# Three rotating PSUM banks for the attention scores, with the bank of the K and V projections given up, in an attention and feed-forward layer on eight cores

## The chip, the cores and the metric

The kernel runs on the 8 cores of one Trainium2 chip. Each core computes two of the sixteen sequences with the same program, and no core talks to another. The metric is the device time of the slowest core in microseconds (us).

## The reference

```python
# x: (16, 2048, 1024); 16 query heads, 2 key/value heads of 64
q = (x @ Wq + bq).reshape(b, s, 16, 64).transpose(0, 2, 1, 3)
k = (x @ Wk + bk).reshape(b, s, 2, 64).transpose(0, 2, 1, 3)
v = (x @ Wv + bv).reshape(b, s, 2, 64).transpose(0, 2, 1, 3)
kp, vp = pad(k, 128 zeros on both sides), pad(v, likewise)
# position i sees the 256 padded positions i .. i+255
scores = einsum('bgrsd,bgswd->bgrsw', qg, k_win)
probs  = softmax(scores, axis=-1)
out    = einsum('bgrsw,bgswd->bgrsd', probs, v_win) @ Wo + bo
x = layernorm(x + out)
# complex linear layer, W_real and W_imag (512 x 512) unfolded from small factors
out_real = x_real @ W_real.T - x_imag @ W_imag.T + bias_real
out_imag = x_real @ W_imag.T + x_imag @ W_real.T + bias_imag
x = layernorm(x + concatenate([out_real, out_imag], axis=-1))
```

## The kernel before

**Order of the work.** One Python function, `schedule`, is run once for each engine and emits that engine's instructions in the order in which the units are called. Every engine therefore executes the same list of units in order, each taking from it only its own part. Synchronisation is by counting semaphores: a unit waits for the count that an earlier unit left under a name in `E.res(...)` or `E.ev[...]`. An instruction that waits holds up everything behind it on its engine.

**Stages.** For each of the two sequences (b = 0, 1) of 2048 rows:

- `emit_qkv(b, q)` handles 512 rows. It loads x in four blocks of 128 rows, converts them on ACT (L371), transposes them on PE (L381), copies the result with DVE (L391), and makes the queries in eight groups of eight matmuls (L411) into two PSUM banks pW0 and pW1 in turn, each evicted by ACT (L420). Then come the keys (L434, evicted at L440) and the values (L447, evicted at L454), both in the single bank pB, and four small transposes of the values (L464, L470). It is called for q = 0 and 1 ahead of the loop, for q = 2 at the end of iteration 5 and for q = 3 at the end of iteration 9: 8 calls in all.
- The main loop runs over k = 0 to 17, one block of 128 rows per iteration, as a software pipeline of three blocks: scores and exponentials of block S = k, attention output and its projection of block P = k - 1, feed-forward layer of block k - 2.

**One iteration on PE**: scores (0,0); values quad 0; scores (0,1); values quad 1; transposes of x1 (L735); feed-forward half 0 (L764); scores (1,0); values quad 2; feed-forward half 1; scores (1,1); values quad 3; transposes of the attention output (L612); scores (2,0); projection half 0 (L637); scores (2,1); projection half 1. The pair in brackets is (c, pair): c is one of three blocks of keys, pair one of two groups of heads.

**The score units.** `sc_unit` (L505) is two matmuls of 64 rows by 512 columns, one for each key/value head, in rows 0 to 63 and 64 to 127 of the array, into the banks pS0 and pS1. Each of the two waits for the exponential that last read its bank, the one of the unit just before. The unit signals once, at its second matmul. `exp_unit` (L523) is two ACT activations of 128x512, the first on pS0, the second on pS1; the first of them waits for the unit's signal. `av_unit` (L562) uses pS2 and pS3, which DVE empties (`recip_unit` L580, `normts_unit` L590).

**What stands on ACT between iterations.** `rstd1_unit` (L697, L702) computes the reciprocal deviation of the first layer norm of block P at the end of the iteration, from statistics that DVE makes (L680, L650 to L660) out of both projection halves. On ACT it stands ahead of the exponentials (0,0) of the next iteration. `x1norm_unit` (L715, DVE) follows it, and the transposes L735 of the next iteration wait for that.

**PSUM.** All 8 banks are in use: pS0 to pS3, pW0 and pW1, pB, pT.

Of the kernel before, what the change touches and what calls it, by code (L numbers as in the profile page):

```python
# [7 lines left out]
F32 = mybir.dt.float32  # L8
BF16 = mybir.dt.bfloat16
AF = mybir.ActivationFunctionType  # L10
# [4 lines left out]
TQ = 512  # L15
# [3 lines left out]
def build_nc(debug=False):  # L19
    nc = bass.Bass("TRN2", target_bir_lowering=False)  # L20
# [41 lines left out]
    KT = sb("KT", [128, 2304], BF16)  # L62
    VB = sb("VB", [128, 18 * 130], BF16)
    EX = sb("EX", [128, 24 * 512], BF16)
    vstage = sb("vstage", [128, 512], BF16)
# [14 lines left out]
    wk_sb = sb("wk_sb", [128, 1024], BF16)  # L80
    wv_sb = sb("wv_sb", [128, 1024], BF16)
# [7 lines left out]
    bk_sb = sb("bk_sb", [128, 1], F32)  # L89
    bv_sb = sb("bv_sb", [128, 1], F32)  # L90
# [4 lines left out]
    expbias = sb("expbias", [128, 1], F32)  # L95
# [16 lines left out]
    f2s = sb("f2s", [128, 512], BF16)  # L112
    wstage = [sb("wstage0", [128, D], F32)]

    pS = [nc.alloc_psum_tensor(f"pS{i}", [128, 512], F32).ap() for i in range(4)]
    pW = [nc.alloc_psum_tensor(f"pW{i}", [128, 512], F32).ap() for i in range(2)]
    pB = nc.alloc_psum_tensor("pB", [128, 512], F32).ap()
    pT = nc.alloc_psum_tensor("pT", [128, 1024], BF16).ap()

    SEMS = ["t", "s", "v", "g", "dc", "db", "dw0", "dw1", "dx0", "dx1", "do0", "do1"]  # L120
# [34 lines left out]
    def ap3(base_ap, offset, dims):  # L155
        return AP(base_ap.tensor, offset, dims)

    def schedule(E):
# [195 lines left out]
        def emit_qkv(b, q):  # L354
# [43 lines left out]
            def rhsXT(c):  # L398
                return ap3(XT, c * 128, [[4096, 128], [1024, 4], [1, 128]])

            ev_xt_ready = E.res("XT")["r"]
            for t in range(8):
# [22 lines left out]
                if t == 7:  # L425
                    rqt["r"] = ev_ev
                    rqt["f"] = None
            rb = E.res("pB")
            if cur == "t":
                E.wait(rb["f"])  # L430
                if b == 0 and q == 0:
                    E.wait(wconv_ev["wv"])
            for c in range(8):
                i = ten.matmul(pB[:, :], wk_sb[:, c * 128:(c + 1) * 128], rhsXT(c),  # L434
                               start=(c == 0), stop=(c == 7)) if cur == "t" else None
            ev_mm = E.inc("t", i if cur == "t" else None)
            if cur == "s":
                E.wait(ev_mm)
                E.wait(E.res("KTfree")["f"])
                i = sca.add(KT[:, 128 + q * TQ: 128 + (q + 1) * TQ], pB[:, :], bk_sb[:])  # L440
            ev_kev = E.inc("s", i if cur == "s" else None)
            rb["f"] = ev_kev
            E.res(f"KT{q}")["r"] = ev_kev
            if cur == "t":
                E.wait(rb["f"])
            for c in range(8):
                i = ten.matmul(pB[:, :], wv_sb[:, c * 128:(c + 1) * 128], rhsXT(c),  # L447
                               start=(c == 0), stop=(c == 7)) if cur == "t" else None
            ev_vmm = E.inc("t", i if cur == "t" else None)
            E.res("XTfree")["f"] = ev_vmm  # L450
            if cur == "s":
                E.wait(ev_vmm)
                E.wait(E.res("vstage")["f"])
                i = sca.add(vstage[:], pB[:, :], bv_sb[:])  # L454
            ev_vev = E.inc("s", i if cur == "s" else None)
            rb["f"] = ev_vev
            rpt = E.res("pT")
            ev_vbev = None
            for T in range(4):
# [17 lines left out]
            E.res(f"VB{q}")["r"] = ev_vbev  # L477

        quadcol = {0: 0, 1: 512, 2: 256, 3: 768}

        def sc_unit(b, S, c, pair):
            parity = (S // 4) % 2
            kb = S - 1 + c
            qready = E.res(f"QT{parity}")["r"]
            kready = E.res(f"KT{S // 4}")["r"]
            knext = E.res(f"KT{min(S // 4 + 1, 3)}")["r"]
            i = None
            for gq in range(2):
                quad = pair * 2 + gq
                rowbase = 64 * gq  # L490
                tilegrp = pair * 2048
                if cur == "t":
                    if gq == 0:
                        if b == 0 and S == 0 and c == 0:
                            E.wait(ev_init_v)
                        if debug and b == 0 and S in (1, 2) and c == 0 and pair == 0:
                            E.wait(E.ev.get("dbg0"))
                        E.wait(qready)
                        E.wait(kready)
                        E.wait(knext)  # L500
                    E.wait(E.res(f"scb{quad % 2}")["f"])
                rhs = ap3(QT, rowbase * 8192 + parity * 4096 + tilegrp
                          + (S % 4) * 128, [[8192, 64], [512, 4], [1, 128]])
                lhsT = KT[rowbase:rowbase + 64, (kb + 1) * 128:(kb + 2) * 128]
                i = ten.matmul(pS[quad % 2][:, :], lhsT, rhs, start=True, stop=True,  # L505
                               tile_position=(rowbase, 0)) if cur == "t" else None
            ev_sc = E.inc("t", i if cur == "t" else None)
            E.ev[f"sc_{S % 2}_{c}_{pair}"] = ev_sc
            if S % 4 == 3 and c == 2 and pair == 1:
                E.res(f"QT{parity}")["f"] = ev_sc  # L510

        def exp_unit(b, S, c, pair):
            ev_sc = E.ev[f"sc_{S % 2}_{c}_{pair}"]
            for gq in range(2):
                quad = pair * 2 + gq
                exi = (S % 2) * 12 + c * 4 + quad
                rex = E.res(f"exfree{exi}")
                if cur == "s":
                    if b == 0 and S == 0 and c == 0 and pair == 0 and gq == 0:
                        sca.wait_ge(SEMH["v"], ev_init_v[1])  # L520
                    E.wait(ev_sc)
                    E.wait(rex["f"])
                    i = sca.activation(EX[:, exi * 512:(exi + 1) * 512],  # L523
                                       pS[quad % 2][:, :], AF.Exp, bias=expbias[:])
                ev_e = E.inc("s", i if cur == "s" else None)
                E.ev[f"exp_{S % 2}_{c}_{quad}"] = ev_e
                if gq == 1:
                    E.res(f"scb0")["f"] = E.ev[f"exp_{S % 2}_{c}_{pair * 2}"]
                    E.res(f"scb1")["f"] = ev_e

        def mask_unit(b, S, c, pair):
            m = maskl if c == 0 else maskr
# [10 lines left out]

        def av_unit(b, S, quad):
            g = quad % 2
            bank = 2 + quad % 2
            vready = E.res(f"VB{S // 4}")["r"]
            vnext = E.res(f"VB{min(S // 4 + 1, 3)}")["r"]
            if cur == "t":
                E.wait(E.res(f"avb{quad % 2}")["f"])  # L550
                E.wait(vready)
                E.wait(vnext)
                for c in range(3):
                    key = ("msk" if c != 1 else "exp") + f"_{S % 2}_{c}_{quad}"
                    E.wait(E.ev[key])
            first = True
            i = None
            for c in range(3):
                kb = S - 1 + c
                exi = (S % 2) * 12 + c * 4 + quad  # L560
                for hh in range(4):
                    i = ten.matmul(  # L562
                        pS[bank][:, hh * 65:(hh + 1) * 65],
                        EX[:, exi * 512 + hh * 128: exi * 512 + (hh + 1) * 128],
                        VB[:, (kb + 1) * 130 + g * 65: (kb + 1) * 130 + (g + 1) * 65],
                        start=first, stop=(c == 2 and hh == 3)) if cur == "t" else None
                    first = False
            ev = E.inc("t", i if cur == "t" else None)
            E.ev[f"av_{S % 2}_{quad}"] = ev
            for c in range(3):  # L570
                E.res(f"exfree{(S % 2) * 12 + c * 4 + quad}")["f"] = ev

        def recip_unit(b, S, quad):
            ring = S % 2
            i = None
            if cur == "v":
                E.wait(E.ev[f"av_{S % 2}_{quad}"])
                if quad == 0:
                    E.wait(E.res(f"attn{ring}")["f"])
                i = vec.reciprocal(Rrec[:, ring * 16 + quad * 4: ring * 16 + (quad + 1) * 4],  # L580
                                   ap3(pS[2 + quad % 2], 64, [[512, 128], [65, 4]]))
            E.inc("v", i)

        def normts_unit(b, S, quad):
            ring = S % 2
            bank = 2 + quad % 2
            E.bar("v")
            i = None
            for hh in range(4):
                i = vec.tensor_scalar(  # L590
                    attn[:, ring * 1024 + quadcol[quad] + hh * 64:
                         ring * 1024 + quadcol[quad] + (hh + 1) * 64],
                    ap3(pS[bank], hh * 65, [[512, 128], [1, 64]]),
                    Rrec[:, ring * 16 + quad * 4 + hh: ring * 16 + quad * 4 + hh + 1],
                    None, ALU.mult) if cur == "v" else None
            ev_nq = E.inc("v", i)
            E.res(f"avb{quad % 2}")["f"] = ev_nq
            if quad == 3:
                E.res(f"attn{ring}")["r"] = ev_nq
                E.ev[f"nq_{ring}"] = ev_nq  # L600
# [403 lines left out]
```

How the kernel before makes its waits and increments, by code:

```python
        def bar(self, name):  # L139
            if self.cur == name:
                self.h.wait_ge(SEMH[name], self.c[name])
# [1 line left out]
        def wait(self, ev):  # L143
            if ev is None:
                return
            if isinstance(ev, list):
                for e in ev:
                    self.wait(e)
                return
            self.h.wait_ge(SEMH[ev[0]], ev[1])
# [7 lines left out]
    def schedule(E):  # L158
# [3 lines left out]
        vec = E.h if cur == "v" else None  # L162
        gps = E.h if cur == "g" else None
        syn = E.h if cur == "sync" else None
        if cur == "v":
            vec.memset(expbias[:], -32.0)
            vec.memset(neghalf[:], -0.5)
            vec.memset(ones_row[:], 1.0)
            i = vec.memset(VB[:], 0.0)
            i.then_inc(SEMH["v"], 1)
            vec.wait_ge(SEMH["v"], E.c["v"] + 1)
            vec.memset(ap3(VB, 64, [[2340, 128], [130, 18]]), 1.0)
            vec.memset(ap3(VB, 129, [[2340, 128], [130, 18]]), 1.0)
            vec.memset(KT[:, 0:128], 0.0)
# [22 lines left out]
        E.inc("db", i, 16)  # L198
        i = syn.dma_start(brow_st[0:1, :], bo_d.rearrange("(o f) -> o f", o=1)) \
            if cur == "sync" else None
        ev_bo = E.inc("db", i, 16)
        if cur == "s":
            sca.wait_ge(SEMH["db"], ev_bo[1])
            i = sca.copy(bo_row[:], brow_st[:])
        ev_borow = E.inc("s", i if cur == "s" else None)
        if cur == "sync":
            syn.wait_ge(SEMH["s"], ev_borow[1])
        i = syn.dma_start(brow_st[0:1, 0:512], br_d.rearrange("(o f) -> o f", o=1)) \
```

## Time and profile before

| | |
|---|---|
| runs of the kernel before | 1432.85 and 1475.86 us, median 1454.35 |
| profiled execution, its own time | 1431.67 us |
| its span, slowest core (core 3) | 1430.1 us |
| spans of the eight cores | 1425.3 to 1430.1 us |
| mean granted TensorE clock | 0.737 to 0.739 of full speed on all cores |
| PE busy / DVE / ACT / POOL | 60% / 37% / 28% / 25% of the span |

The span runs from the first to the last instruction of the slowest core. The engines are PE (TensorE matmul), PEld (its weight loads), DVE (VectorE), ACT (ScalarE), POOL (GpSimd) and SP. In a row of the timeline the first number is the start and the second the duration, both in us, "x2" is a count of merged instructions, and the bracket gives the idle time of the engine just before and the instruction that ended it.

### The profile page before, as it was taken

How to read it: one execution, taken by the hardware profiler on the slowest of the kernel's cores; microseconds unless marked ns; L12 is line 12 of the kernel's file. 1: busy time of each engine (PE TensorE's matmuls, PEld its weight loads, DVE VectorE, ACT ScalarE, POOL GpSimd, SP SyncE). 2: the span in 40 equal slices, each digit the busy share in tenths (PEclk: the TensorE clock that was granted, in tenths of full speed). 3: DMA queues.
4: the chain of work that ended last, by engine and by line, in shares of the span. 5: the costliest groups of instructions: out<-in, count | busy, mean ns of one | idle time of the engine just before them, and what ended most of it. 6: DMA issues, size and time to landing. Idle time of an engine off the chain costs nothing.

```text
span 1430.1 us, 17008 instructions; the slowest of 8 cores (1425.3 to 1430.1 us)
## 1 busy us (share of the span) xinstructions
PE 863.3 (60%) x4568; PEld 354.3 (25%) x4568; DVE 532.2 (37%) x1539; ACT 397.0 (28%) x673; POOL 357.8 (25%) x324
## 2 busy tenths in 40 slices
PE   0077334675586666676756576667577658666664
PEld 0033001222232223222222232222232223222221
DVE  0010444355414551444554111454425441455443
ACT  2332113223223223323220234322232322322210
POOL 0000004243213340333430104343214321333410
PEclk9997555677677677777676686767787767767676
DMA  4510000000200011000000300000200020000000
GB/s 128 177 66 24 0 1 0 1 27 18 74 1 16 16 34 55 16 16 15 15 31 15 104 30 1 15 16 16 74 1 30 15 74 1 15 16 30 15 16 30
DMA packets 15869, 44.51 MB, mean 31 GB/s; under 512 B 3091, under 2 KB 5539, under 8 KB 15782
## 3 DMA queue, kind: packets, MB, share of 16 engines
q0 software_dynamic: 9216, 33.56, 6.4%
q1 hardware_dynamic: 6566, 9.87, 2.4%
q8 instruction: 45, 0.74, 0.2%
q14 instruction: 42, 0.34, 0.1%
HBM read 26.65 MB, written 16.78 MB: 30 GB/s over the span
## 4 chain that ended last, share of the span: by engine, by line
PE 54%; DVE 19%; issue 11%; DMA 7%; ACT 6%; POOL 2%; DVEq 1%; SPq 0%; ACTq 0%; POOLq 0%
PE pW L764 12%; PE pW L637 11%; PE pW L411 9%; PE pS L505 5%; PE pS L562 4%; DVE scr L650 4%; DVE attn L590 4%; DMA xs<-x 4%; PE pT L735 2%; ACT EX L523 2%; PE pW L641 2%; PE pW L768 2%; DVE pre L783 2%; PE pT L612 2%; DVE pre L680 1%
## 5 line engine op out<-in xcount | busy, mean ns | idle before, releaser
L523 ACT ACTIVATE EX<-pS,expbias 128x512 bf16<-128x512 f32 x384 | 243.0, 684 | 395.5 <-PE pS L505 395.2
L539 POOL TENSOR_TENSOR EX<-EX,maskr_s 128x512 bf16<-128x512 bf16 x128 | 172.2, 1368 | 358.8 <-ACT EX L523 358.2
L539 POOL TENSOR_TENSOR EX<-EX,maskl_s 128x512 bf16<-128x512 bf16 x128 | 149.5, 1196 | 383.4 <-ACT EX L523 383.3
L637 PE MATMUL pW<-wo_sb,attnT 128*128 128x512 bf16 x512 | 180.3, 516 | 37.1 <-DVE pre L783 35.9
L505 PE MATMUL pS<-QT,KT 64*128 64x512 bf16 x384 | 120.4, 490 | 122.1 <-ACT EX L523 120.3
L411 PE MATMUL pW<-XT,wq_sb 128*128 128x512 bf16 x512 | 129.5, 420 | 8.9 <-DVE XT L391 8.9
L381 PE MATMUL pT<-identb,x_tm 128*128 128x128 bf16 x256 | 31.6, 301 | 150.5 <-ACT x_tm L371 134.3
L590 DVE TENSOR_SCALAR attn<-pS,Rrec 128x64 bf16<-128x64 f32 x512 | 110.2, 278 | 14.3 <-DVE attn L590 0.5
L764 PE MATMUL pW<-wrt,x1T 128*128 128x512 bf16 x256 | 92.5, 500 | 36.8 <-DVE Rrec L580 34.6
L650 DVE SCALAR_TENSOR_TENSOR scr<-pre 128x1024 bf16<-128x1024 f32 x64 | 102.3, 1598 | 6.7
L580 DVE RECIPROCAL Rrec<-pS 128x4 f32<-128x4 f32 x128 | 19.6, 172 | 205.8 <-PE pS L562 205.8
L637 PEld LDWEIGHTS pW<-wo_sb,attnT 128*128 128x128 bf16 x512 | 57.3, 122 | 142.3 <-issue 123.6
L562 PE MATMUL pS<-VB,EX 128*128 128x65 bf16 x1536 | 82.5, 213 | 5.5 <-POOL EX L539 2.2
L470 DVE COPY VB<-pT 128x128 bf16<-128x128 bf16 x32 | 7.3, 228 | 191.9 <-PE pT L464 191.9
L562 PEld LDWEIGHTS pS<-VB,EX 128*128 128x128 bf16 x1536 | 66.5, 109 | 46.6 <-issue 46.6
L420 ACT ACTIVATE QT<-pW,bq_sb 128x512 bf16<-128x512 f32 x64 | 44.1, 688 | 113.9 <-PE pW L411 113.9
L411 PEld LDWEIGHTS pW<-XT,wq_sb 128*128 128x128 bf16 x512 | 53.6, 106 | 83.0 <-issue 34.5
L612 PE MATMUL pT<-identb,attn 128*128 128x128 bf16 x256 | 23.6, 246 | 79.9 <-DVE attn L590 79.9
L391 DVE COPY XT<-pT 128x1024 bf16<-128x1024 bf16 x32 | 22.1, 691 | 133.0 <-PE pT L381 133.0
L505 PEld LDWEIGHTS pS<-QT,KT 64*128 64x128 bf16 x384 | 24.3, 97 | 189.6 <-issue 187.2
L680 DVE SCALAR_TENSOR_TENSOR pre<-pW,x_tm 128x512 f32<-128x512 f32 x64 | 44.0, 687 | 52.8 <-PE pW L641 52.8
L381 PEld LDWEIGHTS pT<-identb,x_tm 128*128 128x128 bf16 x256 | 24.1, 135 | 157.6 <-issue 157.6
(81 smaller groups left out, 787.6 us busy)
## 6 DMA issues: line engine op xcount, KB each, us to landing
xs<-x POOLq DMA_DIRECT2D x32, 512.0 KB, 4.4
y<-outst POOLq DMA_DIRECT2D x32, 512.0 KB, 3.0
wstage<-wq SPq DMA_DIRECT2D x4, 512.0 KB, 4.2
xs<-wq SPq DMA_DIRECT2D x4, 512.0 KB, 4.8
wstage<-wo SPq DMA_DIRECT2D x4, 512.0 KB, 4.1
xs<-wo SPq DMA_DIRECT2D x4, 512.0 KB, 4.1
wstage<-wk SPq DMA_DIRECT2D x1, 512.0 KB, 5.3
xs<-wv SPq DMA_DIRECT2D x1, 512.0 KB, 4.9
```

What stands on the lines that cost most here:

```text
L381: i = ten.transpose(pT[:, c * 128:(c + 1) * 128], x_tm[:, slot * D + c * 128: slot * D + (c + 1) * 128], identb[:]) if cur == "t" else None
L411: i = ten.matmul(pW[bank][:, :], wq_sb[:, c * 1024 + t * 128: c * 1024 + (t + 1) * 128], rhsXT(c), start=(c == 0), stop=(c == 7)) \
L505: i = ten.matmul(pS[quad % 2][:, :], lhsT, rhs, start=True, stop=True, tile_position=(rowbase, 0)) if cur == "t" else None
L523: i = sca.activation(EX[:, exi * 512:(exi + 1) * 512], pS[quad % 2][:, :], AF.Exp, bias=expbias[:])
L539: i = gps.tensor_mul(EX[:, exi * 512:(exi + 1) * 512], EX[:, exi * 512:(exi + 1) * 512], m[:]) \
L562: i = ten.matmul(pS[bank][:, hh * 65:(hh + 1) * 65], EX[:, exi * 512 + hh * 128: exi * 512 + (hh + 1) * 128], VB[:, (kb + 1) * 130 + g * 6 ...
L590: i = vec.tensor_scalar(attn[:, ring * 1024 + quadcol[quad] + hh * 64: ring * 1024 + quadcol[quad] + (hh + 1) * 64], ap3(pS[bank], hh * 65 ...
L612: i = ten.transpose(pT[:, c * 128:(c + 1) * 128], attn[:, ring * 1024 + c * 128: ring * 1024 + (c + 1) * 128], identb[:]) if cur == "t" el ...
L637: ten.matmul(pW[half][:, :], attnT[:, ring * 1024 + c * 128: ring * 1024 + (c + 1) * 128], wo_sb[:, c * 1024 + half * 512: c * 1024 + (hal ...
L650: lambda: vec.scalar_tensor_tensor(scr[:], pre_getter(), 1.0, pre_getter(), ALU.mult, ALU.mult, accum_out=stt[:, c0 + 2:c0 + 3]),
L680: i = vec.scalar_tensor_tensor(pre1[:, ring * 1024 + half * 512: ring * 1024 + (half + 1) * 512], pW[half][:, :], 1.0, x_tm[:, slot * D + ...
L764: ten.matmul(pW[half][:, :], x1T[:, ring * 1024 + c * 128: ring * 1024 + (c + 1) * 128], wsrc[:, wc * 512:(wc + 1) * 512], start=(c == 0), ...
```

## The change

The eight PSUM banks are divided in another way. Before: two for scores, two for the attention output, two for projections and feed-forward, one for K and V, one for transposes. After: three for scores (pSC0 to pSC2), two for the attention output (pAV0 and pAV1, the former pS2 and pS3), pW0 and pW1, and pT.

- Score unit number u, counted through the program, writes banks 2u mod 3 and (2u + 1) mod 3. So its first matmul goes to the bank which the second exponential of unit u - 2 read (number the matmuls in a row: each takes the bank of the third one before it, where it took that of the second one before it). Its second matmul takes the bank of the first exponential of unit u - 1.
- In `emit_qkv` the keys go to pW0 and the values to pW1. The keys wait for the eviction of query group 6, the values for that of query group 7, and no longer for the eviction of the keys. The users of pW0 and pW1 that follow wait for the evictions of the keys and the values.

No instruction is added or removed, and each engine's instructions stand in the order in which they stood. The rest of the diff renames.

```diff
@@ -112,9 +112,9 @@
     f2s = sb("f2s", [128, 512], BF16)
     wstage = [sb("wstage0", [128, D], F32)]
 
-    pS = [nc.alloc_psum_tensor(f"pS{i}", [128, 512], F32).ap() for i in range(4)]
+    pSC = [nc.alloc_psum_tensor(f"pSC{i}", [128, 512], F32).ap() for i in range(3)]
+    pAV = [nc.alloc_psum_tensor(f"pAV{i}", [128, 512], F32).ap() for i in range(2)]
     pW = [nc.alloc_psum_tensor(f"pW{i}", [128, 512], F32).ap() for i in range(2)]
-    pB = nc.alloc_psum_tensor("pB", [128, 512], F32).ap()
     pT = nc.alloc_psum_tensor("pT", [128, 1024], BF16).ap()
 
     SEMS = ["t", "s", "v", "g", "dc", "db", "dw0", "dw1", "dx0", "dx1", "do0", "do1"]
...
@@ -425,35 +425,36 @@
                 if t == 7:
                     rqt["r"] = ev_ev
                     rqt["f"] = None
-            rb = E.res("pB")
+            rb = E.res("pW0")
             if cur == "t":
                 E.wait(rb["f"])
                 if b == 0 and q == 0:
                     E.wait(wconv_ev["wv"])
             for c in range(8):
-                i = ten.matmul(pB[:, :], wk_sb[:, c * 128:(c + 1) * 128], rhsXT(c),
+                i = ten.matmul(pW[0][:, :], wk_sb[:, c * 128:(c + 1) * 128], rhsXT(c),
                                start=(c == 0), stop=(c == 7)) if cur == "t" else None
             ev_mm = E.inc("t", i if cur == "t" else None)
             if cur == "s":
                 E.wait(ev_mm)
                 E.wait(E.res("KTfree")["f"])
-                i = sca.add(KT[:, 128 + q * TQ: 128 + (q + 1) * TQ], pB[:, :], bk_sb[:])
+                i = sca.add(KT[:, 128 + q * TQ: 128 + (q + 1) * TQ], pW[0][:, :], bk_sb[:])
             ev_kev = E.inc("s", i if cur == "s" else None)
             rb["f"] = ev_kev
             E.res(f"KT{q}")["r"] = ev_kev
+            rb1 = E.res("pW1")
             if cur == "t":
-                E.wait(rb["f"])
+                E.wait(rb1["f"])
             for c in range(8):
-                i = ten.matmul(pB[:, :], wv_sb[:, c * 128:(c + 1) * 128], rhsXT(c),
+                i = ten.matmul(pW[1][:, :], wv_sb[:, c * 128:(c + 1) * 128], rhsXT(c),
                                start=(c == 0), stop=(c == 7)) if cur == "t" else None
             ev_vmm = E.inc("t", i if cur == "t" else None)
             E.res("XTfree")["f"] = ev_vmm
             if cur == "s":
                 E.wait(ev_vmm)
                 E.wait(E.res("vstage")["f"])
-                i = sca.add(vstage[:], pB[:, :], bv_sb[:])
+                i = sca.add(vstage[:], pW[1][:, :], bv_sb[:])
             ev_vev = E.inc("s", i if cur == "s" else None)
-            rb["f"] = ev_vev
+            rb1["f"] = ev_vev
             rpt = E.res("pT")
             ev_vbev = None
             for T in range(4):
...
@@ -477,16 +478,19 @@
             E.res(f"VB{q}")["r"] = ev_vbev
 
         quadcol = {0: 0, 1: 512, 2: 256, 3: 768}
+        scu_ctr = [0]
 
         def sc_unit(b, S, c, pair):
             parity = (S // 4) % 2
             kb = S - 1 + c
+            u = scu_ctr[0]
+            scu_ctr[0] += 1
+            banks = ((2 * u) % 3, (2 * u + 1) % 3)
             qready = E.res(f"QT{parity}")["r"]
             kready = E.res(f"KT{S // 4}")["r"]
             knext = E.res(f"KT{min(S // 4 + 1, 3)}")["r"]
             i = None
             for gq in range(2):
-                quad = pair * 2 + gq
                 rowbase = 64 * gq
                 tilegrp = pair * 2048
                 if cur == "t":
...
@@ -498,19 +502,19 @@
                         E.wait(qready)
                         E.wait(kready)
                         E.wait(knext)
-                    E.wait(E.res(f"scb{quad % 2}")["f"])
+                    E.wait(E.res(f"pSC{banks[gq]}")["f"])
                 rhs = ap3(QT, rowbase * 8192 + parity * 4096 + tilegrp
                           + (S % 4) * 128, [[8192, 64], [512, 4], [1, 128]])
                 lhsT = KT[rowbase:rowbase + 64, (kb + 1) * 128:(kb + 2) * 128]
-                i = ten.matmul(pS[quad % 2][:, :], lhsT, rhs, start=True, stop=True,
+                i = ten.matmul(pSC[banks[gq]][:, :], lhsT, rhs, start=True, stop=True,
                                tile_position=(rowbase, 0)) if cur == "t" else None
             ev_sc = E.inc("t", i if cur == "t" else None)
-            E.ev[f"sc_{S % 2}_{c}_{pair}"] = ev_sc
+            E.ev[f"sc_{S % 2}_{c}_{pair}"] = (ev_sc, banks)
             if S % 4 == 3 and c == 2 and pair == 1:
                 E.res(f"QT{parity}")["f"] = ev_sc
 
         def exp_unit(b, S, c, pair):
-            ev_sc = E.ev[f"sc_{S % 2}_{c}_{pair}"]
+            ev_sc, banks = E.ev[f"sc_{S % 2}_{c}_{pair}"]
             for gq in range(2):
                 quad = pair * 2 + gq
                 exi = (S % 2) * 12 + c * 4 + quad
...
@@ -521,12 +525,10 @@
                     E.wait(ev_sc)
                     E.wait(rex["f"])
                     i = sca.activation(EX[:, exi * 512:(exi + 1) * 512],
-                                       pS[quad % 2][:, :], AF.Exp, bias=expbias[:])
+                                       pSC[banks[gq]][:, :], AF.Exp, bias=expbias[:])
                 ev_e = E.inc("s", i if cur == "s" else None)
                 E.ev[f"exp_{S % 2}_{c}_{quad}"] = ev_e
-                if gq == 1:
-                    E.res(f"scb0")["f"] = E.ev[f"exp_{S % 2}_{c}_{pair * 2}"]
-                    E.res(f"scb1")["f"] = ev_e
+                E.res(f"pSC{banks[gq]}")["f"] = ev_e
 
         def mask_unit(b, S, c, pair):
             m = maskl if c == 0 else maskr
...
-            bank = 2 + quad % 2
+            bank = quad % 2
...
-                        pS[bank][:, hh * 65:(hh + 1) * 65],
+                        pAV[bank][:, hh * 65:(hh + 1) * 65],
```

## Rows read from the trace of the kernel before

**Rows 1.** The page's first part: busy time, share of the span, instructions.
```profile
PE 863.3 (60%) x4568; PEld 354.3 (25%) x4568; DVE 532.2 (37%) x1539; ACT 397.0 (28%) x673; POOL 357.8 (25%) x324
```
**Rows 2.** Waits of the whole span: who waited for whom, us, times, longest us.
```profile
ACT EX L523 <- PE pS L505: 395.2, 165, 7.9
...
PE pS L505 <- ACT EX L523: 120.3, 44, 5.3
...
PE pT L612 <- DVE attn L590: 79.9, 32, 2.8
...
PE pB L447 <- ACT KT L440: 7.7, 8, 1.0
```
**Rows 3.** Timeline from iteration 11 into 12: all engines, start, duration, what.
```profile
621.19 3.57 PE L637 MATMUL pW<-wo_sb,attnT 128*128 128x512 bf16 x8 [1.07 <-DVE pre L783]
...
625.23 0.61 PE L505 MATMUL pS<-QT,KT 64*128 64x512 bf16 x2
...
625.77 1.90 PE L637 MATMUL pW<-wo_sb,attnT 128*128 128x512 bf16 x8
...
627.92 0.39 PE L505 MATMUL pS<-QT,KT 64*128 64x512 bf16 x2
...
628.96 1.98 DVE L650 SCALAR_TENSOR_TENSOR scr<-pre 128x1024 bf16<-128x1024 f32 x1
...
632.45 0.30 ACT L702 ACTIVATE rstd<-st,neghalf 128x1 f32<-128x1 f32 x1
632.65 1.25 ACT L523 ACTIVATE EX<-pS,expbias 128x512 bf16<-128x512 f32 x2
632.99 0.81 DVE L715 TENSOR_SCALAR x_tm<-pre,st,rstd 128x1024 bf16<-128x1024 f32 x1 [0.93 <-ACT rstd L702]
...
633.47 1.16 PE L505 MATMUL pS<-QT,KT 64*128 64x512 bf16 x2 [4.69 <-ACT EX L523]
...
634.73 0.82 PE L562 MATMUL pS<-VB,EX 128*128 128x65 bf16 x12
...
635.36 1.04 PE L735 MATMUL pT<-identb,x_tm 128*128 128x128 bf16 x8
```
**Rows 4.** Timeline of iteration 0, where PE has only score units.
```profile
233.79 1.27 ACT L523 ACTIVATE EX<-pS,expbias 128x512 bf16<-128x512 f32 x2 [0.82 <-PE pS L505]
234.62 1.16 PE L505 MATMUL pS<-QT,KT 64*128 64x512 bf16 x2 [0.93 <-ACT EX L523]
...
235.88 1.27 ACT L523 ACTIVATE EX<-pS,expbias 128x512 bf16<-128x512 f32 x2 [0.82 <-PE pS L505]
...
237.97 0.69 ACT L523 ACTIVATE EX<-pS,expbias 128x512 bf16<-128x512 f32 x1 [0.82 <-PE pS L505]
```
**Rows 5.** Timeline of the keys and values in `emit_qkv(0, 2)`.
```profile
411.70 1.89 PE L434 MATMUL pB<-XT,wk_sb 128*128 128x512 bf16 x8
412.01 0.69 ACT L420 ACTIVATE QT<-pW,bq_sb 128x512 bf16<-128x512 f32 x1 [1.04 <-PE pW L411]
413.69 0.69 ACT L440 ACTIVATE KT<-pB,bk_sb 128x512 bf16<-128x512 f32 x1 [0.98 <-PE pB L434]
414.52 1.89 PE L447 MATMUL pB<-XT,wv_sb 128*128 128x512 bf16 x8 [0.93 <-ACT KT L440]
416.56 0.69 ACT L454 ACTIVATE vstage<-pB,bv_sb 128x512 bf16<-128x512 f32 x1 [2.18 <-PE pB L447]
```
**Rows 6.** Four iterations: stretch, its length, busy us per engine, PEclk (granted clock), DMA.
```profile
603.70:632.45 28.75, 19.07 (x112) 7.76 (x112) 14.60 (x44) 8.49 (x17) 10.78 (x9) 0.76 0.05 19
632.45:661.66 29.21, 20.28 (x112) 8.09 (x112) 13.64 (x44) 8.50 (x17) 10.78 (x9) 0.71 0.05 19
661.66:690.35 28.69, 19.07 (x112) 7.72 (x112) 14.55 (x44) 8.49 (x17) 10.78 (x9) 0.76 0.05 19
690.35:719.83 29.48, 20.29 (x112) 8.15 (x112) 13.64 (x44) 8.49 (x16) 10.78 (x9) 0.71 0.05 19
```

More of the change, by code:

```diff
@@ L580, in recip_unit @@
                 i = vec.reciprocal(Rrec[:, ring * 16 + quad * 4: ring * 16 + (quad + 1) * 4],
-                                   ap3(pS[2 + quad % 2], 64, [[512, 128], [65, 4]]))
+                                   ap3(pAV[quad % 2], 64, [[512, 128], [65, 4]]))
             E.inc("v", i)
@@ L585, in normts_unit @@
             ring = S % 2
-            bank = 2 + quad % 2
+            bank = quad % 2
             E.bar("v")
@@ L592, in normts_unit @@
                          ring * 1024 + quadcol[quad] + (hh + 1) * 64],
-                    ap3(pS[bank], hh * 65, [[512, 128], [1, 64]]),
+                    ap3(pAV[bank], hh * 65, [[512, 128], [1, 64]]),
                     Rrec[:, ring * 16 + quad * 4 + hh: ring * 16 + quad * 4 + hh + 1],
```

## The prediction

> **What bounds the kernel now.** I read the shares of the page first, then the table of waits, then the timeline of one iteration of the loop, of the first iteration and of one projection stage, and last the loop's iterations side by side. No engine is full: PE has the most work, 60% of the span, then DVE with 37% [rows 1]. So the time is a chain through several engines, and what matters is which waits PE, the longest member of it, runs into. ACT waits 395.2 us for scores, but that only says that it is idle; PE waits 120.3 us, 44 times, for an exponential to free a score bank, 79.9 us, 32 times, for the attention output, and 7.7 us, 8 times, in the projections for the eviction of the keys [rows 2]. The change touches the first and the last of these three.
>
> The 44 waits are of few kinds. In a normal iteration five of the six score units find their banks free, because other matmuls stand between them. Only unit (0,1) waits: in the timeline PE has finished the scores (0,0) that started at 627.92 and its values quad, and then stands idle 4.69 us until 633.47 [rows 3]. The reader is to see why: the exponentials (0,0) start only at 632.65, behind the reciprocal deviation at 632.45 on ACT, which waits for the statistics of DVE (the squares start at 628.96), which wait for the second projection half. This chain holds back both exponentials of (0,0), and the change leaves all of it alone. In iteration 0 there is nothing between the score units, and each waits 0.93 us for the exponentials of the unit before [rows 4].
>
> **What the third bank does at the wait.** Before, matmul one of unit (0,1) waits for exponential one, and matmul two for exponential two. Exponential one takes 0.69 us (the last row of [rows 4]), from 632.65 to 633.3; matmul one starts at 633.47 [rows 3]. The pair of exponentials takes 1.27 in place of 0.69 [rows 4], so the second ends 0.58 after the first, and the pair of matmuls takes 1.16 us [rows 3], that is, 0.58 and another 0.58 one behind the other. After, matmul one has a bank that has been free for long, and is done during the idle time, while matmul two waits for exponential one alone. It then starts where matmul one started. The end of the unit comes 0.58 us earlier. The main part of the wait, the 4.69 us here, stays.
>
> That one matmul is what remains, and not two, can be seen where nothing waits: there the pair takes 0.61 us at the lower clock and 0.39 at the higher [rows 3], so two matmuls cost hardly more than one, and no further gain is to be had from separating them. The Trainium skill states this as a rule (TensorE: Matmul & The Clock Gate, section "Packing small matmuls"): matmuls in different row groups of the array run side by side. By that rule the waits of the second matmul are what made 1.16 out of 0.61, and the trace agrees.
>
> **Is the 0.58 us on the path?** Behind the unit stand values quad 1 (634.73), the transposes of x1 (635.36), DVE's copy and the feed-forward half. The transposes also wait for DVE's L715, which ends at 632.99 + 0.81 = 633.80 [rows 3]. Started 0.58 earlier they would begin at 634.78, still some 0.98 after that, so this wait doesn't become the later one. All that follows in the iteration (attention output, projection, statistics) hangs on PE and moves with it. The reciprocal deviation of the next iteration therefore comes 0.58 earlier too, and the gain adds up from iteration to iteration. Iterations with both scores and a preceding reciprocal deviation are k = 2 to 15, in two sequences 28: 28 x 0.58 = 16.2 us. Below, this could be 0 (if another wait covers it); above, 0.69 for each, a whole exponential: 19.3 us.
>
> **Iteration 0 and the start of 1.** A round of unit and exponentials takes 235.88 - 233.79 = 2.09 us [rows 4]: 1.27 of exponentials and 0.82 of idle ACT. After, matmul two starts at the end of exponential one instead of two, so the round shortens by 0.58 as well, to 1.51. Such waits are 6 per sequence (five in iteration 0, one at the start of iteration 1), 12 x 0.58 = 7.0 us. In iteration 1 two further units per sequence stand behind values quads, which partly cover the wait; between 0 and 0.58 each, I take half, 4 x 0.3 = 1.2 us. POOL's masks also come earlier here; POOL is 25% busy [rows 1] and I cost them at nothing.
>
> **Keys and values.** The values' matmuls start 0.93 us after those of the keys have ended, because the keys' eviction (413.69, 0.69 us) must empty the bank [rows 5]. With a bank of its own this wait goes: 7.7 us over 8 calls [rows 2]. What comes late next? The keys need the eviction of query group 6; the one of group 7 starts at 412.01 and that of group 6 stood before it on ACT, while the keys start at 411.70, so group 6 is out by then. The values need group 7, out at 412.70, while the keys' matmuls run until 413.59. The eviction of the keys ends at 414.38, well before the values' would be due (their 8 matmuls take 1.89), so ACT is not in the way. PE goes straight on, ACT's eviction of the values and all that follows move up. The gain is 7.7 us, between 0 (if the projections were bound by loads of x) and 8.7 (0.16 us more per call, if the drawn end of the last matmul also overlaps). The feed-forward and projection units that use pW0 and pW1 next come much later, so the new waits there cost nothing.
>
> **Sum.** 16.2 + 7.0 + 1.2 + 7.7 = 32.1 us. The profiled execution took 1431.67 us, 1.6 more than its span, so 1431.7 - 32.1 = 1399.6, which I round to 1399. The median of the runs shown, 1454.35, is of two that lie 43 us apart; the profiled execution agrees with the lower, 1432.85, and I measure against these two. The gain is 2.2%, just over the 2% that a measurement of this kernel can tell from no change; that line is at 1403 us.
>
> **The clock.** The loop doesn't run at one clock. Eight projection matmuls take 3.57 us at the lower level (1.2 GHz) and, half an iteration later, 1.90 at the higher (2.4 GHz) [rows 3]. Iterations with a mean granted clock of 0.76 take 28.75 and 28.69 us, those with 0.71 take 29.21 and 29.48 [rows 6], in turn. A shift of 0.58 us per iteration changes where the clock rises and falls against the work. The mean of the four is 29.03. If all became like the better ones (28.72) there would be 28 x 0.31 = 9 us more gain; if all became like the worse (29.35), 9 us less. No row says which, so these are two cases.
>
> **The rivals.**
> 1. The clock turns for the worse: 1399.6 + 9 = 1408. For it: the alternation shows that the length of an iteration and the clock hang together. Against: PE has less idle time than before, not more.
> 2. The clock turns for the better: 1391. For it: the idle stretch before unit (0,1) gets a matmul inside it.
> 3. The wait is only exchanged: exponential two is freed from the chain, but in the loop values quad 1 or the transposes find another wait (a mask of POOL, L715), and only iterations 0 and 1 and the projections gain: 1431.7 - 7.0 - 1.2 - 7.7 = 1416. For it: the attention output's wait stays at 2.5 us per iteration (79.9 / 32 [rows 2]), and the masks stand on an engine of their own, whose order PE's waits depend on. Against: the margin of 0.98 us worked out above.
> 4. Slower: the clock falls where it did not. If the new timing leaves one more group of eight matmuls of 512 columns at 1.2 GHz in each iteration, it costs 3.57 - 1.90 = 1.67 us, 28 x 1.67 = 46.8 us, and the time is 1399.6 + 46.8 = 1446; with two groups 1493. It decides from 32.1 / 28 = 1.15 us per iteration on, five or six such matmuls at the lower clock. For it: PE still waits twice in each iteration for more than 2 us, and the waits are where the clock falls. Against: the two waits stay in place and one gets no longer. The Trainium skill speaks for this rival (the same page, section "A second HAM failure mode: psum-queue depth-cycling"): in a kernel that cycles through PSUM banks, short idle times between groups made the clock swing, and throughput suffered. The trace has the swing already with two banks, 0.76 and 0.71 in turn.
>
> **How the numbers follow.** The forecast with its own spread of a few us has 0.53, rival 2 has 0.14, rival 1 has 0.18, rival 3 has 0.10, rival 4 has 0.05, 0.02 of it with two groups. The range has to leave out rival 4 and may cut the outer parts of 2 and 3: below 1384 lies only a clock case with the upper bounds (19.3, 8.7, and 0.58 for the four covered units, 37.4 in all, and 9 more: 1385), above 1417 the slower one. Faster by over 2% are rival 2 and most of the forecast, together 0.60, as its own spread reaches over 1403; slower by over 2% is rival 4 with two groups, 0.02; the rest, 0.38, is within 2%.
>
> **What would show each step right or wrong.** Right: the waits of the score matmuls for exponentials stay at 4 to 5 us in the loop, but the matmul behind the wait stands alone, and values quad 1 starts 0.6 us after it and not 1.26; the rounds of iteration 0 take 1.5 us; the row of the values' wait for the keys is gone; iterations take about 28.4 us at an unchanged mix of clock. Wrong: the transposes L735 or values quad 1 show a new idle time of 0.5 us (rival 3), or the mean clock of the iterations leaves 0.71 to 0.76 (rivals 1, 2 and 4).

## The result and the profile after

| | before | after |
|---|---|---|
| median of the runs | 1434.16 us (10 runs) | 1400.15 us (11 runs) |
| profiled execution, its span | 1431.67 us, 1430.1 us | 1400.15 us, 1398.6 us |
| mean granted clock of the cores | 0.737 to 0.739 | 0.738 to 0.744 |

In some executions of any kernel the cores of one die have a lower granted clock and the time is some per cent longer (two of the ten runs before, 1475.86 and 1470.67 us); the ratios here leave these out. The ratio of the changed kernel to the one before is 0.9777, 95% interval 0.9751 to 0.9803. The kernel became 2.2% faster. The interval reaches past the 2% line (0.98), so it isn't settled that the gain is over 2%; the forecast had put it just over that line.

The page of the changed kernel, first part: busy time and share of the span.

```profile
PE 846.5 (61%) x4568; PEld 353.8 (25%) x4568; DVE 539.5 (39%) x1539; ACT 396.2 (28%) x673; POOL 357.8 (26%) x324
```

PE is 17 us less busy than in [rows 1], 9 of them in the score matmuls (120.4 us in the page before, 111.0 after). DVE is 7 us more busy with the same instructions. That was not foreseen, and comes back below.

The waits of the changed kernel (engine and line, who was waited for, us in total, times, longest), as answer to [rows 2]:

```profile
ACT EX L527 <- PE pSC L509: 366.8, 159, 7.9
...
PE pSC L509 <- ACT EX L527: 111.9, 36, 5.5
...
PE pT L614 <- DVE attn L592: 80.1, 32, 2.8
```

The row of the values' wait for the keys' eviction is gone. The waits of score matmuls for exponentials have shrunk only from 120.3 to 111.9 us: the third bank hardly shortens the wait, it takes work out from behind it. A reader who measures this change by the table of waits alone would see 8 us of it.

The timeline of the changed kernel from one iteration to the next, as answer to [rows 3]:

```profile
611.24 0.39 PE L509 MATMUL pSC<-QT,KT 64*128 64x512 bf16 x2
...
611.64 2.27 POOL L541 TENSOR_TENSOR EX<-EX,maskr_s 128x512 bf16<-128x512 bf16 x2
612.03 0.39 PE L509 MATMUL pSC<-QT,KT 64*128 64x512 bf16 x1
...
612.29 2.71 DVE L652 SCALAR_TENSOR_TENSOR scr<-pre 128x1024 bf16<-128x1024 f32 x1
...
616.51 0.29 ACT L704 ACTIVATE rstd<-st,neghalf 128x1 f32<-128x1 f32 x1
616.71 1.25 ACT L527 ACTIVATE EX<-pSC,expbias 128x512 bf16<-128x512 f32 x2
617.05 0.81 DVE L717 TENSOR_SCALAR x_tm<-pre,st,rstd 128x1024 bf16<-128x1024 f32 x1 [0.93 <-ACT rstd L704]
...
617.52 0.58 PE L509 MATMUL pSC<-QT,KT 64*128 64x512 bf16 x1 [5.10 <-ACT EX L527]
618.21 0.82 PE L564 MATMUL pAV<-VB,EX 128*128 128x65 bf16 x12
...
618.84 1.04 PE L737 MATMUL pT<-identb,x_tm 128*128 128x128 bf16 x8
```

Matmul one of unit (0,1) runs from 612.03 to 612.42, at the start of what was idle time. Only matmul two stands behind the wait, and values quad 1 follows 0.69 us after its start, where it was 634.73 - 633.47 = 1.26 us. The difference is 0.57 us.

Iteration 0, as answer to [rows 4]:

```profile
229.26 1.27 ACT L527 ACTIVATE EX<-pSC,expbias 128x512 bf16<-128x512 f32 x2 [0.24 <-PE pSC L509]
230.09 1.16 PE L509 MATMUL pSC<-QT,KT 64*128 64x512 bf16 x2 [0.35 <-ACT EX L527]
230.77 1.27 ACT L527 ACTIVATE EX<-pSC,expbias 128x512 bf16<-128x512 f32 x2 [0.25 <-PE pSC L509]
```

A round takes 230.77 - 229.26 = 1.51 us in place of 2.09. The "x2" of 1.16 us merges matmul two of one unit with matmul one of the next. The second of them starts 0.58 us behind the first, at 230.67, because its bank is emptied by exponential two, which ends at 229.26 + 1.27 = 230.53. It is done by 231.25, ahead of the end of the next exponential one (230.77 + 0.69 = 231.46), so it adds nothing to the round.

Keys and values, as answer to [rows 5]:

```profile
401.12 1.89 PE L434 MATMUL pW<-XT,wk_sb 128*128 128x512 bf16 x8
401.43 0.69 ACT L420 ACTIVATE QT<-pW,bq_sb 128x512 bf16<-128x512 f32 x1 [1.04 <-PE pW L411]
402.84 1.89 PE L448 MATMUL pW<-XT,wv_sb 128*128 128x512 bf16 x8
403.11 0.69 ACT L440 ACTIVATE KT<-pW,bk_sb 128x512 bf16<-128x512 f32 x1 [0.98 <-PE pW L434]
404.89 0.69 ACT L455 ACTIVATE vstage<-pW,bv_sb 128x512 bf16<-128x512 f32 x1 [1.09 <-PE pW L448]
```

The values start 1.72 us after the keys, where it was 2.82: 1.10 us per call, 8.8 for eight.

Iterations of the changed kernel (length, busy us per engine, granted clock, DMA), as answer to [rows 6]:

```profile
616.51:644.60 28.09, 19.32 (x112) 7.69 (x112) 14.14 (x44) 8.48 (x16) 10.78 (x9) 0.73 0.05 19
644.60:672.71 28.11, 19.00 (x112) 7.78 (x112) 14.57 (x44) 8.48 (x16) 10.77 (x9) 0.76 0.05 20
672.71:701.65 28.94, 18.83 (x112) 7.98 (x112) 14.89 (x44) 8.48 (x17) 10.77 (x9) 0.74 0.05 20
```

These three follow another pattern than the four before (two short ones and a long one, not short and long in turn), and their mean is 28.38 us against 29.03. Over all 24 iterations without projections the granted clock is 0.740 against 0.738 before.

**Where the 31.5 us of span went.** I split both spans at the reciprocal deviations (L702 before, L704 after):

| stretch | before | after | gain |
|---|---|---|---|
| start to the first one (two projections, iterations 0 and 1) | 266.54 | 258.64 | 7.9 |
| 24 iterations without projections | 695.9 | 681.9 | 14.0 |
| 4 iterations with projections | 266.6 | 260.0 | 6.6 |
| between the sequences (two projections, iterations 0 and 1) | 125.26 | 120.83 | 4.4 |
| iteration 16 of each sequence, and the end | 75.9 | 77.3 | -1.4 |

An iteration gained 14.0 / 24 = 0.58 us. One with a projection gained 1.65, which is 0.58 + 1.10 within rounding. These are the slowest cores, core 3 before and core 5 after. The medians of the eight cores gained 6.2, 12.8, 8.9, 6.1 and 0.8 us in the five stretches: 0.53 us per iteration, and no loss at the end, so the -1.4 belongs to this core.

### The profile page after: what moved, and what is told of

It is laid out like the page before. It is cut to its first block, busy times and chain, and to the rows that moved or that the text cites. A ratio compares the mean times of both kernels' runs of the same rounds, so it can differ in the third digit from the quotient of the medians.

```text
span 1398.6 us, 17008 instructions; the slowest of 8 cores (1388.6 to 1398.6 us)
## 1 busy us (share of the span) xinstructions
PE 846.5 (61%) x4568; PEld 353.8 (25%) x4568; DVE 539.5 (39%) x1539; ACT 396.2 (28%) x673; POOL 357.8 (26%) x324
## 4 chain that ended last, share of the span: by engine, by line
PE 53%; DVE 20%; issue 11%; DMA 7%; ACT 6%; DVEq 1%; POOL 1%; SPq 0%; ACTq 0%; POOLq 0%
PE pW L766 12%; PE pW L639 11%; PE pW L411 9%; DVE scr L652 5%; PE pSC L509 4%; PE pAV L564 4%; DMA xs<-x 4%; DVE attn L592 4%; PE pT L737 2%; ACT EX L527 2%; DVE pre L785 2%; PE pW L770 2%; PE pT L614 2%; PE pW L643 2%; DVE pre L682 1%
## 5 line engine op out<-in xcount | busy, mean ns | idle before, releaser
L527 ACT ACTIVATE EX<-pSC,expbias 128x512 bf16<-128x512 f32 x384 | 242.7, 683 | 367.5 <-PE pSC L509 366.8
L509 PE MATMUL pSC<-QT,KT 64*128 64x512 bf16 x384 | 111.0, 468 | 113.2 <-ACT EX L527 111.9
L592 DVE TENSOR_SCALAR attn<-pAV,Rrec 128x64 bf16<-128x64 f32 x512 | 110.2, 278 | 14.3 <-DVE attn L592 0.5
L652 DVE SCALAR_TENSOR_TENSOR scr<-pre 128x1024 bf16<-128x1024 f32 x64 | 109.2, 1707 | 6.7
L582 DVE RECIPROCAL Rrec<-pAV 128x4 f32<-128x4 f32 x128 | 19.7, 173 | 195.7 <-PE pAV L564 195.7
L564 PE MATMUL pAV<-VB,EX 128*128 128x65 bf16 x1536 | 81.3, 211 | 7.7 <-issue 2.4
L564 PEld LDWEIGHTS pAV<-VB,EX 128*128 128x128 bf16 x1536 | 65.3, 108 | 47.2 <-issue 47.2
L509 PEld LDWEIGHTS pSC<-QT,KT 64*128 64x128 bf16 x384 | 23.9, 95 | 171.8 <-issue 167.3
```

The costliest lines, as they stand in the source:

```text
L509: i = ten.matmul(pSC[banks[gq]][:, :], lhsT, rhs, start=True, stop=True, tile_position=(rowbase, 0)) if cur == "t" else None
L527: i = sca.activation(EX[:, exi * 512:(exi + 1) * 512], pSC[banks[gq]][:, :], AF.Exp, bias=expbias[:])
L564: i = ten.matmul(pAV[bank][:, hh * 65:(hh + 1) * 65], EX[:, exi * 512 + hh * 128: exi * 512 + (hh + 1) * 128], VB[:, (kb + 1) * 130 + g * ...
L592: i = vec.tensor_scalar(attn[:, ring * 1024 + quadcol[quad] + hh * 64: ring * 1024 + quadcol[quad] + (hh + 1) * 64], ap3(pAV[bank], hh * 6 ...
L652: lambda: vec.scalar_tensor_tensor(scr[:], pre_getter(), 1.0, pre_getter(), ALU.mult, ALU.mult, accum_out=stt[:, c0 + 2:c0 + 3]),
```

## The experiments

All ten were compared with the kernel before on the same chip, which took 1433 to 1436 us there; each ratio is to it.

**One part at a time.** First the third score bank alone:

```diff
-            rb1 = E.res("pW1")
+            rb1 = E.res("pW0")
...
-                i = ten.matmul(pW[1][:, :], wv_sb[...
+                i = ten.matmul(pW[0][:, :], wv_sb[...
```

Expected: 

> The changed kernel, but keys and values share the bank pW0, so that the values wait for the keys' eviction again; the three score banks stay. If the two parts of the change add up: in the changed kernel values start 1.72 us after keys, before 2.82 us, so 8 x 1.10 = 8.8 us come back, 1400.2 + 8.8 = 1409 us. Rival (the projections were not on the path, all of the gain is in the loop and the first iteration): 1400 to 1402.

Measured: 1410.51 us, ratio 0.9829 (0.9785 to 0.9872). Then the keys' and values' banks alone:

```diff
-            banks = ((2 * u) % 3, (2 * u + 1) % 3)
+            banks = (0, 1)
```

Expected: 

> The changed kernel with two score banks only, as before; keys and values in pW0 and pW1. If the parts add up: 1434.2 - 8.8 = 1425 us, the waits of the score matmuls back to matmul pairs of 1.16 us behind each wait and rounds of 2.09 us in iteration 0. Rival (the gain of the third bank was in truth one of the clock, which any small shift gives): 1410 or less.

Measured: 1425.31 us, ratio 0.9917 (0.989 to 0.9945). The parts give 1.7% and 0.8%, in sum 2.5% against 2.2% for both; within the intervals they add up. Each lies at the value worked out from rows, 1409 and 1425.

The two parts don't act on separate things alone. In the 24 iterations without projections the granted clock was 0.728 in this run, 0.738 in the kernel before and 0.740 in the changed one, and PE's matmuls other than the scores were busy 16.7, 16.5 and 16.4 us per iteration. So of the 1425.3 - 1400.2 = 25 us that the third bank is worth on top of the other part, some 7 (0.3 x 24, an estimate from these busy times) are work at a better clock. Against the kernel before the loop's clock hardly moved.

**The same banks, exchanged within a unit.** This asks whether it is the third bank as such that helps, or which exponential releases it.

```diff
-            banks = ((2 * u) % 3, (2 * u + 1) % 3)
+            banks = ((2 * u + 1) % 3, (2 * u) % 3)
```

Expected: 

> Three score banks, but the two banks of each unit exchanged: the first matmul takes the bank that the unit before's second exponential reads, the second takes the free bank. By my theory the gain comes from waiting for exponential one in place of two, with one matmul left behind the wait. Here the wait is for exponential two, and the pair of matmuls (0.6 us side by side) follows: 0.58 + 0.58 as with two banks. So it should read like two score banks, about 1425 us, with rounds near 2.09 us in iteration 0. Rival (any third bank helps, or a shifted clock does it): about 1400 us.

Measured: 1429.03 us, ratio 0.9965 (0.9944 to 0.9987), even 4 us over the kernel with two banks. Its timeline in iteration 0:

```profile
236.13 0.72 PE L509 MATMUL pSC<-QT,KT 64*128 64x512 bf16 x2 [1.51 <-ACT EX L527]
236.95 1.27 ACT L527 ACTIVATE EX<-pSC,expbias 128x512 bf16<-128x512 f32 x2 [0.96 <-PE pSC L509]
...
238.36 0.71 PE L509 MATMUL pSC<-QT,KT 64*128 64x512 bf16 x2 [1.51 <-ACT EX L527]
```

The pair now stands side by side, 0.72 us, but behind the second exponential. A round takes 2.23 us in place of the 2.09 that were expected: what is left behind exponential two is the pair's 0.72 us, where with two banks it was matmul two's 0.58. Whether that makes all of the 4 us isn't shown. Three banks with the wrong rotation are worth nothing. The gain is in the release by exponential one, with matmul one out of the way.

**Why DVE is more busy.** The squares of the first layer norm (L650, after: L652; one DVE instruction that squares 1024 columns and sums them, with both inputs in SBUF) stand in the chain ahead of the loop's wait. On the median of the eight cores the 32 of them take 59.0 us in the changed kernel and 53.6 in the one before. I left out the masks which POOL applies to unit (2,1), and with them that part of the computation:

```diff
                     exp_unit(b, S, 2, 1)
-                    mask_unit(b, S, 2, 1)
+                    for quad in (2, 3):
+                        E.ev[f"msk_{S % 2}_2_{quad}"] = E.ev[f"exp_{S % 2}_2_{quad}"]
```

Expected: 

> The changed kernel without POOL's masks of unit (2,1) (32 x 2 multiplications left out, so quads 2 and 3 attend to keys beyond the window's right end). It tests what lengthens DVE's squares of the first layer norm, which stand in the chain ahead of the loop's wait: 62.2 us for 32 in the changed kernel, 1.23 us each at the shortest, and 56 us before. If POOL's masks running at the same time do it, all fall to 1.23 us and the loop gains up to 62.2 - 39.4 = 23 us: about 1377 to 1385 us. Rival (something else lengthens them, or the waits behind take it up): 1398 to 1402 us.

Measured: 1376.63 us, ratio 0.9578 (0.9552 to 0.9605); all 32 squares of the first layer norm take 1.23 us. The rows say how it works. In the changed kernel POOL's two masks end at 611.64 + 2.27 = 613.91, and the squares, begun at 612.29, end at 615.00, 1.09 us after POOL. Without a mask beside them they take 1.23. So the squares don't share with the masks, they stand still until POOL is done. The Trainium skill says so (SBUF — State Buffer, section "SBUF: two separate sides"): VectorE and GpSimd have one pair of SBUF ports in common, which either a DVE instruction with two SBUF inputs or a GpSimd instruction that reads SBUF holds for its whole length, while the other is blocked. The trace agrees that one stands still for the other. By the page the pair goes to whichever starts first; here the squares started at 612.29, the second mask at 612.76, and the second mask still went ahead, so that what counts for the squares is when both masks are done.

**The masks kept, but later.** They are needed only in the next iteration.

```diff
                     exp_unit(b, S, 2, 1)
-                    mask_unit(b, S, 2, 1)
...
                     ln1_unit(b, P)
+                if S < 16:
+                    if P >= 0 and cur == "g":
+                        E.wait(E.ev[f"var1_{P % 2}"])
+                    mask_unit(b, S, 2, 1)
```

Expected: 

> The changed kernel with POOL's masks of unit (2,1) put behind the layer norm statistics of the same iteration, all work kept. They are not needed before values quads 2 and 3 of the next iteration. If leaving them out helped because DVE's squares no longer run beside them, moving them gives the same: squares at 1.23 us, about 1377 us. Rival (they slow whatever DVE does next, L717 and the copies, or reach the values quads too late): 1385 us or more, with a new wait of PE for POOL or a longer L717.

Measured: 1394.05 us, ratio 0.9694 (0.9671 to 0.9717). A miss by 17 us, although all squares take 1.23 us and the plain iterations, all but one, 27.1 to 27.8. The stretches with projections have grown, from 65.3, 65.0, 65.0 and 64.7 us to 67.6, 67.8, 69.2 and 71.1. The timeline ahead of such a projection, first of the changed kernel (mask, loads issued, conversion on ACT):

```profile
366.95 2.26 POOL L541 TENSOR_TENSOR EX<-EX,maskr_s 128x512 bf16<-128x512 bf16 x2
...
369.15 1.13 POOL L363 DMA_DIRECT2D xs<-x  x2
...
374.14 1.04 ACT L371 CAST x_tm<-xs 128x1024 bf16<-128x1024 f32 x1 [2.03 <-DMA xs<-x]
```

and of this one:

```profile
369.88 1.59 POOL L541 TENSOR_TENSOR EX<-EX,maskr_s 128x512 bf16<-128x512 bf16 x1
371.41 1.13 POOL L363 DMA_DIRECT2D xs<-x  x2
376.20 1.04 ACT L371 CAST x_tm<-xs 128x1024 bf16<-128x1024 f32 x1 [6.97 <-DMA xs<-x]
```

POOL also issues the loads of x. They stood behind the masks that now wait, and ACT was idle 6.97 us for them in place of 2.03.

**The reciprocal deviation out of the way.** In the changed kernel PE still waits 5.10 us at unit (0,1), because on ACT the exponentials (0,0) stand behind it.

```diff
                     exp_unit(b, S, 0, 0)
+                if 0 <= Q2 < 16:
+                    rstd1_unit(b, Q2)
+                    x1norm_unit(b, Q2)
...
                     ln1_unit(b, P)
-                    rstd1_unit(b, P)
-                    x1norm_unit(b, P)
```

Expected: 

> The changed kernel with the reciprocal deviation of the first layer norm (L699, L704 and DVE's L717) emitted behind the exponentials (0,0) of the next iteration in place of ahead of them. If that order is what makes PE wait before unit (0,1), this wait goes, and the next limit is the transposes, which need L717: in the changed kernel L717 ended at 589.20 and they began at 590.18, so about 0.82 us per iteration, 28 x 0.82 = 23 us: 1377 us, with the idle time of some 4 us now ahead of the transposes. Rival (the wait at unit (0,1) is only a place where a chain shows that is as long without it): 1395 to 1402 us.

Measured: 1429.45 us, ratio 0.9955 (0.9939 to 0.9971): 29 us slower than the changed kernel where 23 faster was expected. Its timeline:

```profile
625.31 1.26 ACT L527 ACTIVATE EX<-pSC,expbias 128x512 bf16<-128x512 f32 x2 [1.37 <-PE pSC L509]
...
625.81 4.02 DVE L652 SCALAR_TENSOR_TENSOR scr<-pre 128x1024 bf16<-128x1024 f32 x1
...
626.14 0.37 PE L509 MATMUL pSC<-QT,KT 64*128 64x512 bf16 x1 [0.20 <-ACT EX L527]
626.50 2.25 POOL L541 TENSOR_TENSOR EX<-EX,maskl_s 128x512 bf16<-128x512 bf16 x2
...
632.95 1.01 PE L737 MATMUL pT<-identb,x_tm 128*128 128x128 bf16 x8 [5.59 <-DVE x_tm L717]
```

The exponentials (0,0) are early now, and so are their masks. They follow the masks (2,1) on POOL without a pause, until 628.75, and the squares end 1.08 us later, at 629.83. The wait at unit (0,1) is down to 0.20 us, and the transposes wait 5.59 us instead, as expected; what was not expected are the squares. All 32 take 85.1 us on this core, against 62.2 on the changed kernel's. The old order had, by accident, kept POOL quiet during most of the squares.

**Both together**, the late masks and the moved reciprocal deviation.

Expected: 

> Late masks and the moved reciprocal deviation together. If both shorten the same chain one behind the other (squares, then L717 to the transposes), the gains add up: 1400 - 23 - 23 = 1354 us. If the second only removes what the first leaves idle: 1370 to 1377 us.

Measured: 1404.21 us, ratio 0.9777 (0.9746 to 0.9808). The squares are back at 1.23 us, the plain iterations at 26.8 to 28.7, but the stretches with projections at 70 us. This missed even the higher of the two forecasts by 27 us. It had left out the loads of x, which were not yet understood: the three runs were forecast together. It is also 10 us slower than the late masks alone. Of that 7 us lie in the stretches with projections (medians of the cores: 281.1 us against 274.0), where the moved reciprocal deviation now stands behind the whole projection stage.

**The loads repaired.** In iterations 5 and 9 the masks stay in their old place:

```diff
                     exp_unit(b, S, 2, 1)
+                    if k in (5, 9):
+                        mask_unit(b, S, 2, 1)
...
-                if S < 16:
+                if S < 16 and k not in (5, 9):
```

Expected: 

> As the run with late masks, but in iterations 5 and 9, which are followed by loads of x that POOL issues, the masks stay in their old place. The theory: late masks gave the loop its full gain (iterations of 27.3 us as without these masks), but the stretches with the projections grew from 65.0 us on the mean to 68.9, because the loads of x stood on POOL behind masks that wait for the statistics. Summed over the four stretches 15.6 us: 1394 - 15.6 = 1378 us. Rival (the stretches grew for another reason): 1390 us or more.

Measured: 1377.91 us, ratio 0.9621 (0.9576 to 0.9667), where 1378 was expected; the four stretches are 64.2, 64.2, 65.3 and 63.9 us. With the moved reciprocal deviation added, save in these two iterations:

Expected: 

> The same with the reciprocal deviation moved behind the exponentials (0,0), except ahead of the projections. With the masks of unit (0,0) no longer beside the squares, the move should keep only its gain: the transposes began 5.6 us after the second projection half there, 6.1 with late masks alone, so 0.5 us x 24 = 12 us less: 1366 us. Rival: the loop's iterations were 27.3 us in both, with and without the move, so it gives nothing: 1376 to 1380 us.

Measured: 1373.99 us, ratio 0.9579 (0.9552 to 0.9605). The interval overlaps with that of the run before, so of the move's gain no more can be said than that it is small, between the two theories. This is the fastest version with the full computation: 4.2% under the kernel before and 26 us under the changed one.

**The third bank in that setting.** The repaired version with two score banks:

Expected: 

> Late masks and early loads, but two score banks (keys and values stay in pW0 and pW1). If the third bank is worth the 0.58 us of the second exponential at each wait whatever else is on the chain, it costs what it costs in the changed kernel, 1425.3 - 1400.2 = 25 us: 1378 + 25 = 1403 us, iterations 0.6 us longer. Rival (iterations settle near certain lengths together with the clock, so 27.3 us stays): 1385 to 1390 us.

Measured: 1410.17 us, ratio 0.9836 (0.9808 to 0.9865). The third bank is worth 1410.2 - 1377.9 = 32 us here, more than the 25 expected. Its 24 plain iterations take 28.54 us on the mean against 27.53 with three banks: 1.0 us each, of which 0.58 are the second exponential. In these iterations the granted clock is 0.737 with two banks and 0.748 with three, and PE's matmuls other than the scores, the same in number, are busy 16.6 us against 16.3. So about 0.3 of the other 0.4 us is work at a lower clock. Why the clock is lower there isn't shown.

## Why the prediction was right

- **The step at the wait** (0.58 us, the second exponential) held: 0.57 us in the timeline, 0.58 as mean over 24 iterations. The exchanged banks, which have the same three banks and not this release, gave nothing.
- **The number of such waits** (28 in the loop, 16.2 us) held: 14.0 us in the plain iterations and 6.6 - 4 x 1.10 = 2.2 in those with projections, 16.2 in sum. But this is a net value. The squares of both layer norms took 109.2 us in 64 in place of 102.3, 6.9 us more, 6.4 of them in the first layer norm, whose squares stand beside POOL's masks for longer. The prediction cost the masks at nothing; for iteration 0, where it said so, that held, but in the loop it had not looked at what POOL does to DVE. About as much came back: PE's matmuls other than the scores are 5.4 us less busy with the same instructions. That these two, neither of them foreseen, nearly cancel is luck, and so is the agreement to a tenth of a us; on the medians of the cores the same sum is 12.8 + 8.9 - 4.4 = 17.3 us.
- **Iteration 0 and the start of 1** (7.0 and 1.2 us): a round takes 1.51 us as worked out. The two stretches that hold it gained 7.9 and 4.4 us, less the four projections' 4.4 in sum 7.9 us, against 8.2 forecast. Singly they are 5.7 and 2.2 on these cores, where 4.1 each was forecast; on the medians of the cores they are 4.0 and 3.9.
- **Keys and values** (7.7 us, bound 8.7): 8.8 us. The bound was added up wrongly, 7.7 + 8 x 0.16 is 9.0, and 8.8 lies just inside it. The last matmul's end, drawn beyond the start of the next, was the term that the 7.7 left out. The run with this part alone gave 1425.3 us.
- **Sum**: 32.1 us forecast, 31.5 measured in the profiled execution. Two small misses stand against each other: 1.1 us more in the projections, and 1.4 us lost in the last stretch, for which the forecast had nothing and which the median of the cores doesn't show.
- **The rivals.** The clock (1 and 2): the pattern of the iterations did change, but the granted clock of the 24 iterations went from 0.738 to 0.740 only, and the 5.4 us less of busy time are fewer than the 9 us allowed. Exchanged wait (3): the transposes found no new wait, values quad 1 started 0.69 us behind the single matmul. Slower clock (4), for which the Trainium skill's section on cycling PSUM banks spoke (TensorE: Matmul & The Clock Gate, "A second HAM failure mode: psum-queue depth-cycling"): the mean clock of the cores went from 0.737 to 0.739 up to 0.738 to 0.744, so it did no harm here.

## What to carry to other kernels

Ask of a bank ring which reader releases each bank and what is then left behind the wait. A third bank saved one exponential and one matmul per wait, the same three banks in another rotation nothing, and the table of waits showed little of it. Before an engine's work is moved earlier or later, list everything that runs beside it at the new place: a DVE instruction that reads two SBUF operands stood still here while POOL's masks ran (1.23 us became up to 4.99), and loads of x issued by POOL waited with its masks (16 us in four projection stages).

## What was unexpected of the hardware

Where the squares of the first layer norm begin while masks run on POOL, they end 1.08 to 1.09 us after the last of these masks, whether they take 1.98 us, 2.71 or 4.02. They take 1.23 us when no mask is running as they begin, or when it ends within their first 0.13 us. The profile shows this only as a longer instruction, never as a wait. The masks of the kernel before, beside the squares of [rows 3] that run from 628.96 to 630.94, in its timeline:

```profile
627.59 2.26 POOL L539 TENSOR_TENSOR EX<-EX,maskr_s 128x512 bf16<-128x512 bf16 x2
```

They end at 629.85, 1.09 us ahead of the squares' end. It goes the other way too, at the squares of the second layer norm 7 us earlier:

```profile
621.10 3.24 POOL L539 TENSOR_TENSOR EX<-EX,maskr_s 128x512 bf16<-128x512 bf16 x2 [11.71 <-ACT EX L523]
...
621.76 1.57 DVE L650 SCALAR_TENSOR_TENSOR scr<-pre 128x1024 bf16<-128x1024 f32 x1
```

Here the squares wait for the first mask only, and the second mask ends 1.01 us after the squares (624.34 and 623.33): the two masks take 3.24 us in place of 2.26. What decides whether the squares or the next mask go first isn't shown.

In the kernel before this already cost some 16 us of chain (the first layer norm's 32 squares took 55.8 us there, and 32 x 1.23 = 39.4). Removing the overlap was worth 1400.2 - 1377.9 = 22 us, two thirds of what the change itself gave.
